# Pipelined attention scaling, ternary weights partly on ScalarE, and a per-block tile change in a one-layer transformer kernel

## The chip, the cores and the metric

The kernel runs on the eight cores of one Trainium2 chip. Each core takes half of the 4096 tokens of one of four batch items and computes its 2048 output rows alone; the keys and values of the whole item are computed on both of its cores. There is no exchange between cores. The metric is the device time in microseconds of the slowest core.

## The reference

One transformer layer with post-norm: linear attention, then a feed-forward network with ternary weights. Biases are zero, the norms have no gain.

```python
q = x @ Wq.T + bq;  k = x @ Wk.T + bk;  v = x @ Wv.T + bv   # 16 q heads, 4 kv heads, D = 128
sq, sk = elu(q) + 1, elu(k) + 1
kv = einsum('bhsd,bhse->bhde', sk, v);  k_sum = sk.sum(axis=2)
attn = einsum('bhsd,bhde->bhse', sq, kv) / (einsum('bhsd,bhd->bhs', sq, k_sum)[..., None] + 1e-6)
x = layernorm(x + attn @ Wo.T)
wq = lambda w: sign(w) * (abs(w) >= 0.7 * mean(abs(w)))      # 8192 x 2048 and 2048 x 8192
h = gelu(x @ wq(w1).T + b1, approximate=False)
x = layernorm(x + h @ wq(w2).T + b2)
```

## The kernel before

Each engine has an instruction list that is written in program order by `p.op`; every engine executes its own list strictly in order, and semaphores join them. `vector`, `scalar` and `gpsimd` operations also wait for the one before them on the same engine. Activations lie transposed: 128 of the 2048 model dimensions on the partitions (16 d blocks, `dc`), 512 tokens in the free dimension (4 tiles, `t`). DMAs are issued by SyncE (`dma("sync", ...)`: weights w1, w2, their quantised copies, y1s) and by GpSimd (`dma("gpsimd", ...)`: x, wq, wo, all writes), both in order. In the profile the line of a DMA issue is L192.

The stages, one behind the other:

1. K and V of all 4096 tokens and their product kv (L291 to L335), with part of the *scale jobs* beside it: `emit_scale` loads 512 KB of w1 or w2 and ScalarE sums absolute values (L262), VectorE adds them up (L269).
2. Q projection: 16 head blocks `ic`, 4 tiles `t` each. A block is 16 matmuls (L426), then two VectorE operations (L433, L436), Exp on ScalarE (L440) and an add (L442), which make `sq`. Behind them `emit_qkv(ic - 1, t)` multiplies the `sq` of the head before with kv: two matmuls (L382, and L385 for the norm row), Ln and Exp of that one row on ScalarE (L392, L398: the reciprocal), a matmul that spreads the row over 128 partitions (L401), a copy (L405) and the product (L411), into `arnB`. Eight scale jobs follow each `ic` while there are any, that is behind the first eight.
3. Output projection by 16 d blocks and 4 tiles (L553), residual, sums for the norm; the result y1 goes to DRAM (`y1s`). Then the norm's factors for the 4 tiles (L598 to L634).
4. For each tile `t`, the FFN. First the *first norm*: for each d block load y1s into `x1d`, multiply (L704), add (L710), cast to bf16 (L713). Then the first product, 64 chunks `fc` of 16 matmuls (L742), each followed by Gelu on ScalarE (L750). Then the second product, 16 d blocks of 64 matmuls (L790), each followed by the bias add (L799), the residual (L803) and the sums for the second norm (L810, L812, L817). Then that norm's factors (L820 to L855) and the *output norm*: per d block two VectorE operations (L863, L865), in place in `x1d`, and the DMA to `out`.

In the first tile the weights are quantised just ahead of their matmuls and written to DRAM (`w1q`, `w2q`); the other tiles load them from there. `quant_piece` does 128 x 512 weights: a load into one of four staging buffers, two VectorE operations (L677, L683) that make -1, 0 or 1, and the write. A chunk of w1 is 4 pieces and has two buffers, half a d block of w2 is 8 pieces and has three.

What decides the order around the change is the written order alone, in these places:

```python
            sq_toks[ic][t] = m4_
            if ic >= 1:
                emit_qkv(ic - 1, t)
...
            tld = dma("sync", x1d, y1s[t, dc],
                      waits=[y1_wr[t][dc], x1_free[dc],
                             wo_mm_done if t == 0 else None])
```

`x1_free[dc]` is the output DMA of the tile before: the load of y1s goes into the buffer that this DMA reads.

Of the kernel before, what the change touches and what calls it, by code (L numbers as in the profile page):

```python
# [112 lines left out]
def build_nc():  # L113
# [261 lines left out]
    def emit_qkv(ic, t):  # L375
        nonlocal qkv_free, nrm_free, rbc_free
        kvh = ic // 4
        kv_l = kvsb.ap()[:, kvh * 129: kvh * 129 + 128]
        ks_l = kvsb.ap()[:, kvh * 129 + 128: kvh * 129 + 129]
        sq_t = sq_tile(ic, t)  # L380
        tqkv = p.op("tensor", lambda e, o=PB[2].ap(), l=kv_l, r=sq_t:
                    e.matmul(o, l, r, start=True, stop=True),  # L382
                    waits=[sq_toks[ic][t], t_kv_ev, qkv_free], inc=sT)
        tnrm = p.op("tensor", lambda e, o=PB[3].ap()[0:1, :], l=ks_l, r=sq_t:
                    e.matmul(o, l, r, start=True, stop=True),  # L385
                    waits=[nrm_free], inc=sT)
        qkv_last_mm[ic] = tnrm
        j = (ic * NT + t) % 2
        u_r, r_r = row(0 + j), row(2 + j)
        tu = p.op("scalar", lambda e, o=u_r, a=PB[3].ap()[0:1, :],  # L390
                  b=c_eps_at.ap():
                  e.activation(o, a, AF.Ln, bias=b),  # L392
                  waits=[tnrm, uro[j], st_["c_eps_at"],
                         t_bkr if ic == 0 else None,
                         t_bvr if ic == 0 else None], inc=sC)
        nrm_free = tu
        tr = p.op("scalar", lambda e, o=r_r, a=u_r, s2=c_none.ap():
                  e.activation(o, a, AF.Exp, scale=s2),  # L398
                  waits=[st_["c_none"]], inc=sC)
        tbc = p.op("tensor", lambda e, o=PB[4].ap(), l=ones_k1.ap(), r=r_r:  # L400
# [142 lines left out]
    for dc in range(DC):  # L543
        for t in range(NT):
            par = (dc * NT + t) % 2
            two = None
            for icc in range(16):
# [7 lines left out]
                                  thr_done if (dc == 0 and t == 0) else None],  # L555
# [40 lines left out]
    for t in range(NT):  # L596
# [63 lines left out]
    def quant_piece(which, idx, pc512, dst, dram_dst, dst_waits):  # L660
        first = qres["rr"] == 0
        sl = qres["rr"] % 4
        bl = qres["rr"] % 2
# [12 lines left out]
        tb = p.op("vector", lambda e, o=btile, a=stage, b2=tneg:  # L676
                  e.tensor_single_scalar(o, a, b2, ALU.is_le),  # L677
                  waits=[tok_d, thr_done, qres["b_free"][bl],
                         sqprev if first else None,
                         abs_guard if first else None], inc=sV)  # L680
        qres["lastB"] = tb
        tqv = p.op("vector", lambda e, o=dst, a=stage, s2=tpos, b2=btile:
                   e.scalar_tensor_tensor(o, a, s2, b2, ALU.is_ge, ALU.subtract),  # L683
                   waits=[tb] + list(dst_waits), inc=sV)
# [254 lines left out]
```

How the kernel before makes its waits and increments, by code:

```python
                def go(eng):  # L95
                    for fn, waits, inc in self.ops[ename]:
                        for h, v in waits:
                            eng.wait_ge(h, v)
                        ins = eng.nop() if fn is None else fn(eng)
                        if inc is not None:
                            ins.then_inc(*inc)
```

## Time and profile before

| what | us |
|---|---|
| median of 3 runs | 4919.77 (4708.06 to 4966.57) |
| profiled execution | 4721.89 |
| its span, slowest core (5) | 4720.3 |
| spans of the other cores | 4686.0 to 4713.6 |
| busy PE / DVE / ACT / POOL | 3036.4 / 1587.1 / 730.4 / 420.0 |

The profile is one execution, on the slowest core; a busy time is a sum over all stages. PE is TensorE, DVE VectorE, ACT ScalarE, POOL GpSimd, SP SyncE. L426 is line 426 of the kernel. Matmul ends are modelled, and a sequence that is shown as one row (x16) is 16 instructions in a row.

### The profile page before, as it was taken

The page shows a single profiled execution, that of the slowest core. Times are in us where ns is not written, and L with a number is a line of the kernel's source. Part 1 is how long each engine was busy: PE and PEld are TensorE (multiplying, and loading weights), DVE is VectorE, ACT ScalarE, POOL GpSimd, SP SyncE. Part 2 cuts the span into 40 slices and gives each one's busy share as a digit, 9 for nine tenths or more (in the row PEclk, how much of TensorE's full clock was granted, in tenths as well). Part 3 has the DMA queues.
Part 4 walks back from the last instruction along what each step waited for, and adds up shares of the span by engine and source line. Part 5 has one row for each costly group of instructions (what it writes and reads, how often), then busy time and mean ns, then how long its engine had stood idle before and what let it go on. Part 6 is the DMA issues. An engine that isn't in the chain of part 4 may idle for free.

```text
span 4720.3 us, 40825 instructions; the slowest of 8 cores (4686.0 to 4720.3 us)
## 1 busy us (share of the span) xinstructions
PE 3036.4 (64%) x11722; PEld 1214.4 (26%) x11722; DVE 1587.1 (34%) x2744; ACT 730.4 (15%) x1153; POOL 420.0 (9%) x774
## 2 busy tenths in 40 slices
PE   2455545554776666356664444459995899949996
PEld 0122211111222222022221111124442334414442
DVE  0222222222333333466676656540025001140023
ACT  0344442332121000000000000001100110011100
POOL 1000000000000111022332222200000000000000
PEclk9667777776777888588887777779997999969998
DMA  9755562332011333178885555444443344334442
GB/s 171 177 173 171 178 183 80 89 83 61 13 25 32 98 102 99 60 200 211 222 237 179 180 162 168 144 147 143 156 152 125 125 139 165 134 125 139 156 153 106
DMA packets 215218, 644.51 MB, mean 137 GB/s; under 512 B 30674, under 2 KB 34770, under 8 KB 202708
## 3 DMA queue, kind: packets, MB, share of 16 engines
q1 hardware_dynamic: 161716, 486.66, 34.1%
q0 software_dynamic: 53280, 155.24, 11.7%
q8 instruction: 96, 1.57, 0.1%
q14 instruction: 126, 1.03, 0.1%
HBM read 578.87 MB, written 100.66 MB: 144 GB/s over the span
## 4 chain that ended last, share of the span: by engine, by line
PE 39%; DMA 25%; DVE 20%; ACT 7%; issue 6%; DVEq 1%; POOL 1%; ACTq 0%; SPq 0%; POOLq 0%
PE PB L790 17%; DMA arnE<-w 15%; PE PB L742 13%; PE PB L426 6%; DMA arnE<-xt 6%; DVE arnC L683 5%; DVE arnE L677 3%; ACT arnE L262 3%; DMA arnC<-w1q 2%; PE PB L401 2%; DVEq L98 1%; DVE arnE L433 1%; ACT rows L398 1%; DVE arnB L710 1%; DVE arnB L865 1%
## 5 line engine op out<-in xcount | busy, mean ns | idle before, releaser
L742 PE MATMUL PB<-arnB,arnC 128*128 128x512 bf16 x4096 | 987.9, 399 | 408.1 <-DVE arnC L683 206.4
L790 PE MATMUL PB<-arnA,arnC 128*128 128x512 bf16 x4096 | 939.2, 393 | 301.0 <-DVE arnC L683 301.0
L742 PEld LDWEIGHTS PB<-arnB,arnC 128*128 128x128 bf16 x4096 | 401.7, 101 | 998.6 <-issue 606.9
L790 PEld LDWEIGHTS PB<-arnA,arnC 128*128 128x128 bf16 x4096 | 410.5, 101 | 829.3 <-issue 382.2
L799 DVE TENSOR_SCALAR arnE<-PB,b_sb 128x512 f32<-128x512 f32 x64 | 48.0, 751 | 1370.0 <-PE PB L790 1370.0
L683 DVE SCALAR_TENSOR_TENSOR arnC<-arnE,thr 128x512 bf16<-128x512 f32 x512 | 384.8, 752 | 94.0 <-DVE arnE L677 32.4
L553 PE MATMUL PB<-arnB,arnC 128*128 128x512 bf16 x1024 | 272.7, 429 | 138.7 <-DVE arnE L568 138.7
L426 PE MATMUL PB<-arnA,arnC 128*128 128x512 bf16 x1024 | 336.7, 503 | 11.5 <-DMA arnC<-wq 9.7
L262 ACT ACTIVATE arnE<-arnE 128x1024 bf16<-128x1024 f32 x256 | 270.7, 1057 | 419.8 <-DMA arnE<-w 341.5
L750 ACT ACTIVATE arnA<-PB,b_sb 128x512 bf16<-128x512 f32 x256 | 176.3, 689 | 987.8 <-PE PB L742 987.8
L677 DVE TENSOR_SCALAR arnE<-arnE,thr 128x512 f32<-128x512 f32 x512 | 249.4, 487 | 124.2 <-DMA arnE<-w 78.9
L401 PE MATMUL PB<-rows,ones_k 1*128 1x512 f32 x128 | 94.6, 827 | 293.7 <-ACT rows L398 293.7
L269 DVE SCALAR_TENSOR_TENSOR acc<-acc_t,acc 128x1 f32<-128x1 f32 x256 | 40.8, 159 | 577.8 <-ACT arnE L262 573.5
L812 ACT ACTIVATE arnE<-arnB 128x512 f32<-128x512 f32 x64 | 40.4, 632 | 1206.0 <-DVE arnB L803 1206.0
L335 PE MATMUL PB<-arnG 128*128 128x129 bf16 x128 | 18.7, 301 | 297.1 <-DVE arnG L323 297.1
L426 PEld LDWEIGHTS PB<-arnA,arnC 128*128 128x128 bf16 x1024 | 121.3, 123 | 257.4 <-issue 212.3
L553 PEld LDWEIGHTS PB<-arnB,arnC 128*128 128x128 bf16 x1024 | 106.3, 108 | 306.1 <-issue 223.8
L192 POOL DMA_DIRECT2D out<-arnB x64 | 34.6, 540 | 1639.3 <-DVE arnB L865 1639.2
L192 POOL DMA_DIRECT2D w1q<-arnC x256 | 141.2, 552 | 416.9 <-DVE arnE L677 313.8
L192 POOL DMA_DIRECT2D w2q<-arnC x256 | 138.8, 542 | 434.6 <-DVE arnE L677 395.0
L568 DVE TENSOR_TENSOR arnE<-PB,arnE 128x512 f32<-128x512 f32 x64 | 44.2, 691 | 264.4 <-DMA arnE<-xt 250.2
L192 POOL DMA_DIRECT2D arnC<-wq x16 | 8.4, 528 | 1236.1 <-PE PB L385 654.1
(147 smaller groups left out, 1777.7 us busy)
## 6 DMA issues: line engine op xcount, KB each, us to landing
arnE<-w SPq DMA_DIRECT2D x256, 512.0 KB, 4.3
arnE<-w SPq DMA_DIRECT2D x512, 256.0 KB, 4.2
arnC<-w1q SPq DMA_DIRECT2D x192, 512.0 KB, 3.2
arnC<-w2q SPq DMA_DIRECT2D x96, 1024.0 KB, 5.0
w1q<-arnC POOLq DMA_DIRECT2D x256, 128.0 KB, 4.8
w2q<-arnC POOLq DMA_DIRECT2D x256, 128.0 KB, 3.4
arnE<-xt POOLq DMA_DIRECT2D x64, 256.0 KB, 3.7
y1s<-arnE POOLq DMA_DIRECT2D x64, 256.0 KB, 2.4
```

The costliest lines, as they stand in the source:

```text
L98: eng.wait_ge(h, v)
L192: tok = p.op(qeng, lambda e, a=dst, b=src: e.dma_start(out=a, in_=b), waits=list(waits) + [q["last"][i]], inc=q["lanes"][i], inc_amt=16)
L262: e.activation(Eb9, s2, AF.Abs, accum_out=a2),
L401: e.matmul(o, l, r, start=True, stop=True),
L426: e.matmul(o, l, r, start=s, stop=z),
L553: e.matmul(o, l, r, start=s, stop=z),
L677: e.tensor_single_scalar(o, a, b2, ALU.is_le),
L683: e.scalar_tensor_tensor(o, a, s2, b2, ALU.is_ge, ALU.subtract),
L742: e.matmul(o, l, r, start=s, stop=z),
L750: e.activation(o, a, AF.Gelu, bias=b),
L790: e.matmul(o, l, r, start=s, stop=z),
L799: e.tensor_scalar(o, a, b, None, ALU.add),
```

## The change

1. `emit_qkv` is split. The two matmuls, Ln and Exp stay (new L409, L414, and two ScalarE lines); the spreading matmul (L386), the copy and the product go into `emit_qkv_B`, which is called one block later, behind the next block's 16 matmuls and its VectorE operations. The two PSUM banks of `emit_qkv` become two pairs.
2. In `quant_piece`, one piece in four of w1 and three in eight of w2 take another form: Sign with bias -threshold and Sign with bias +threshold on ScalarE (L704, L708), their sum on VectorE (L711), and Sign of the sum on ScalarE (L713). All other pieces keep the two VectorE operations (L721, L725), with one scratch buffer in place of two. The matmuls wait for the last piece of either form.
3. The bias add of the second product moves from VectorE (L799) to ScalarE.
4. The first norm of tile t+1 is written block by block into the output norm of tile t: behind the two operations and the output DMA of d block `dc` come the load and the three operations (L747, L754, L757) of the same `dc`. Its scratch is Esl(1) instead of Esl(0).

```diff
@@ Q projection: emit_qkv split in two @@
-    qkv_free = nrm_free = rbc_free = None
+    qkv_free = [None, None]
+    nrm_free = [None, None]
+    rbc_free = None
...
+    qkv_pend = []
+    def emit_qkv_B():
+        nonlocal rbc_free
+        if not qkv_pend:
+            return
+        ic, t, qp, j, tqkv, tr = qkv_pend.pop(0)
+        tbc = p.op("tensor", lambda e, o=PB[4].ap(), l=ones_k1.ap(),
+                   r=row(2 + j):
                    e.matmul(o, l, r, start=True, stop=True),
                    waits=[tr, rbc_free], inc=sT)
...
-                   a=PB[2].ap(), b=Esl(0):
+                   a=PB[2 if qp == 0 else 5].ap(), b=Esl(0):
                    e.tensor_mul(o, a, b), waits=[tqkv], inc=sV)
-        qkv_free = tdv
+        qkv_free[qp] = tdv
...
+    def emit_qkv(ic, t):
...
+        qp = (ic * NT + t) % 2
+        tqkv = p.op("tensor", lambda e, o=PB[2 if qp == 0 else 5].ap(),
...
+                    waits=[sq_toks[ic][t], t_kv_ev, qkv_free[qp]], inc=sT)
+        tnrm = p.op("tensor",
+                    lambda e, o=PB[3 if qp == 0 else 6].ap()[0:1, :],
...
+        qkv_pend.append((ic, t, qp, j, tqkv, tr))
...
             sq_toks[ic][t] = m4_
+            emit_qkv_B()
             if ic >= 1:
                 emit_qkv(ic - 1, t)
...
     for t in range(NT):
+        emit_qkv_B()
         emit_qkv(15, t)
+    emit_qkv_B()
@@ quant_piece @@
-        btile = Esl(9) if bl == 0 else Esl(2)
...
+            cform = (pc512 % 4) == 1
...
+            cform = (pc512 % 8) in (1, 4, 6)
...
+        if cform:
...
+            s1 = Eb.ap()[:, 2048:2560]
+            s2 = Eb.ap()[:, 2560:3072]
+            ts1 = p.op("scalar", lambda e, o=s1, a=stage, b=tneg:
+                       e.activation(o, a, AF.Sign, bias=b),
+                       waits=[tok_d, thr_done,
+                              sqprev if firstC else None], inc=sC)
+            ts2 = p.op("scalar", lambda e, o=s2, a=stage, b=tpos:
+                       e.activation(o, a, AF.Sign, bias=b), inc=sC)
+            qres["stage_free"][sl] = ts2
+            tad = p.op("vector", lambda e, o=s1, a=s1, b=s2:
+                       e.tensor_add(o, a, b), waits=[ts2], inc=sV)
+            tqv = p.op("scalar", lambda e, o=dst, a=s1:
+                       e.activation(o, a, AF.Sign),
+                       waits=[tad] + list(dst_waits), inc=sC)
+            qres["lastB"] = tqv
+        else:
...
+            btile = Esl(9)
+            tb = p.op("vector", lambda e, o=btile, a=stage, b2=tneg:
+                      e.tensor_single_scalar(o, a, b2, ALU.is_le),
...
+            tqv = p.op("vector", lambda e, o=dst, a=stage, s2=tpos, b2=btile:
@@ first norm of a tile @@
+    def emit_ln1_dc(t, dc):
+        x1d = Bfap[:, dc * 512:(dc + 1) * 512]
+        x1b = Bbf[:, 16384 + dc * 512: 16384 + (dc + 1) * 512]
+        tld = dma("sync", x1d, y1s[t, dc],
+                  waits=[y1_wr[t][dc], x1_free[dc],
+                         wo_mm_done if t == 0 else None])
+        ta1 = p.op("vector", lambda e, o=Esl(1), a=x1d, b=Abc1(t):
+                   e.tensor_mul(o, a, b),
+                   waits=[tld, ab_done[t],
...
+        ta2 = p.op("vector", lambda e, o=x1d, a=Esl(1), b=Bbc1(t):
+                   e.tensor_add(o, a, b), inc=sV)
+        x1_ready[dc] = ta2
+        x1bf_ready[dc] = p.op("vector", lambda e, o=x1b, a=x1d:
+                              e.tensor_copy(o, a), inc=sV)
...
     for t in range(NT):
-        for dc in range(DC):
...
+        for dc in (range(DC) if t == 0 else []):
+            emit_ln1_dc(t, dc)
@@ bias add of the second product @@
-            tv1 = p.op("vector", lambda e, o=Esl(0), a=PB[2 + par].ap(),
+            tv1 = p.op("scalar", lambda e, o=Esl(0), a=PB[2 + par].ap(),
                        b=b2_sb.ap()[:, dc:dc + 1]:
-                       e.tensor_scalar(o, a, b, None, ALU.add),
-                       waits=[tmm, t_b2], inc=sV)
+                       e.activation(o, a, AF.Identity, bias=b),
+                       waits=[tmm, t_b2, ytmp_free], inc=sC)
@@ output norm @@
             x1_free[dc] = wr
             out_last = wr
             x1_ready[dc] = None
+            if t + 1 < NT:
+                emit_ln1_dc(t + 1, dc)
```

TensorE, Q projection, before (L382 and L385 are the two matmuls of `emit_qkv`, L401 spreads the row, L426 is the projection):

```order
L385 MATMUL PB3<-arnG,kvsb 1x512
L401 MATMUL PB4<-rows,ones_k1 128x512 [waits sC]
L426 MATMUL PB1<-arnA,arnC 128x512 x16
L382 MATMUL PB2<-arnG,kvsb 128x512 [waits sV]
L385 MATMUL PB3<-arnG,kvsb 1x512
L401 MATMUL PB4<-rows,ones_k1 128x512 [waits sC]
```

And now (L409, L414, L386 and L442 in the same roles):

```order
L442 MATMUL PB0<-arnA,arnC 128x512 x16
L386 MATMUL PB4<-rows,ones_k1 128x512 [waits sC,sV]
L409 MATMUL PB2<-arnG,kvsb 128x512 [waits sV]
L414 MATMUL PB3<-arnG,kvsb 1x512
L442 MATMUL PB1<-arnA,arnC 128x512 x16
L386 MATMUL PB4<-rows,ones_k1 128x512 [waits sC,sV]
L409 MATMUL PB5<-arnG,kvsb 128x512 [waits sV]
```

The 16 matmuls of the next block now stand between L409 and L414 and the L386 that belongs to them, and the two PSUM banks take turns with another pair.

ScalarE, first tile's first product, before, from the factors of the first norm to the residual's squares (L750 is Gelu):

```order
L614 ACTIVATE rows<-rows,c_eps_ln 1x512 [waits sV,sC]
L617 ACTIVATE rows<-rows,c_nhalf 1x512 [waits sC]
L750 ACTIVATE arnA<-PB,b_sb 128x512 [waits sT,sC] x64
L812 ACTIVATE arnE<-arnB 128x512 [waits sV,sG1,sC]
L812 ACTIVATE arnE<-arnB 128x512 [waits sV,sC] x15
```

And now (L806 is Gelu, L704 and L708 the two Signs, L713 the last one):

```order
L806 ACTIVATE arnA<-PB,b_sb 128x512 [waits sT,sC]
L704 ACTIVATE arnE<-arnE,thr 128x512 [waits sS2,sC]
L708 ACTIVATE arnE<-arnE,thr 128x512 [waits sC]
L713 ACTIVATE arnC<-arnE 128x512 [waits sV,sG0,sG1,sG2,sG3,sC]
L806 ACTIVATE arnA<-PB,b_sb 128x512 [waits sT,sC]
```

Between any two Gelus there now stand three Signs, of which the first waits for a weight load (sS) and the last for VectorE (sV) and for earlier writes (sG).

VectorE, first tile's first product, before, at its start (L710, L713 end the first norm; L677, L683 are a piece):

```order
L710 TENSOR_TENSOR arnB<-arnE,arnF 128x512 [waits sV]
L713 CAST arnB<-arnB 128x512 [waits sV]
L677 TENSOR_SCALAR arnE<-arnE,thr 128x512 [waits sS1,sV]
L683 SCALAR_TENSOR_TENSOR arnC<-arnE,thr 128x512 [waits sV]
L677 TENSOR_SCALAR arnE<-arnE,thr 128x512 [waits sS2,sV]
L683 SCALAR_TENSOR_TENSOR arnC<-arnE,thr 128x512 [waits sV]
```

And now (L721, L725 are a piece of the kept form, L711 the add of the new one):

```order
L754 TENSOR_TENSOR arnB<-arnE,arnF 128x512 [waits sV]
L757 CAST arnB<-arnB 128x512 [waits sV]
L721 TENSOR_SCALAR arnE<-arnE,thr 128x512 [waits sS1,sV]
L725 SCALAR_TENSOR_TENSOR arnC<-arnE,thr 128x512 [waits sV]
L711 TENSOR_TENSOR arnE<-arnE 128x512 [waits sC,sV]
L721 TENSOR_SCALAR arnE<-arnE,thr 128x512 [waits sS3,sV]
L725 SCALAR_TENSOR_TENSOR arnC<-arnE,thr 128x512 [waits sV]
L721 TENSOR_SCALAR arnE<-arnE,thr 128x512 [waits sS4,sV]
L725 SCALAR_TENSOR_TENSOR arnC<-arnE,thr 128x512 [waits sV]
```

Of each four pieces the second is now the one operation L711, which waits for ScalarE (sC); the third and fourth stand behind it.

VectorE, from the output norm of the first tile to the first norm of the second, before (L863, L865 output norm; L704, L710, L713 first norm):

```order
L863 TENSOR_TENSOR arnE<-arnB,arnE 128x512 [waits sV]
L865 TENSOR_TENSOR arnB<-arnE 128x512 [waits sV]
L704 TENSOR_TENSOR arnE<-arnB,arnF 128x512 [waits sS3,sV]
L710 TENSOR_TENSOR arnB<-arnE,arnF 128x512 [waits sV]
L713 CAST arnB<-arnB 128x512 [waits sV]
L704 TENSOR_TENSOR arnE<-arnB,arnF 128x512 [waits sS4,sV]
```

And now (L928, L930 output norm; L747, L754, L757 first norm):

```order
L928 TENSOR_TENSOR arnE<-arnB,arnE 128x512 [waits sV]
L930 TENSOR_TENSOR arnB<-arnE 128x512 [waits sV]
L747 TENSOR_TENSOR arnE<-arnB,arnF 128x512 [waits sS3,sV]
L754 TENSOR_TENSOR arnB<-arnE,arnF 128x512 [waits sV]
L757 CAST arnB<-arnB 128x512 [waits sV]
L928 TENSOR_TENSOR arnE<-arnB,arnE 128x512 [waits sV]
L930 TENSOR_TENSOR arnB<-arnE 128x512 [waits sV]
```

The three operations of the first norm, with the wait for their load (sS), have moved between the output norms of two neighbouring d blocks.

## Rows read from the trace of the kernel before

**Rows 1.** Busy time by stage: stretch, length, PE, PEld, DVE, ACT, POOL busy (instructions), clock, DMA, GB/s
```profile
...
690.00:1465.00 775.00, 452.43 (x1272) 154.85 (x1272) 239.58 (x401) 202.25 (x320) 9.00 (x17) 0.74 0.22 58
...
2010.00:2490.00 480.00, 296.40 (x1053) 112.83 (x1054) 335.42 (x542) 45.38 (x65) 148.22 (x270) 0.84 0.81 221
...
3366.00:3588.00 222.00, 221.20 (x1025) 100.10 (x1023) 44.00 (x63) 10.16 (x16) 0.00 (x0) 1.00 0.39 143
```

**Rows 2.** Timeline, Q projection: start, us, engine, line, operation, count [idle before <-releaser]
```profile
...
1258.95 0.72 ACT L398 ACTIVATE rows<-rows,c_none 1x512 f32<-1x512 f32 x1
...
1259.82 1.09 PE L401 MATMUL PB<-rows,ones_k 1*128 1x512 f32 x2 [2.92 <-ACT rows L398]
...
1260.84 5.31 PE L426 MATMUL PB<-arnA,arnC 128*128 128x512 bf16 x16
```

**Rows 3.** Chain that ended last, in order of time, Q projection: start, us, what
```profile
...
798.80 6.17 PE PB L426 x16
...
1140.66 5.91 PE PB L426 x16
...
1451.32 5.26 PE PB L426 x16
```

**Rows 4.** Timeline, TensorE, Q projection, end of a burst of scale jobs
```profile
...
907.81 2.04 PE L401 MATMUL PB<-rows,ones_k 1*128 1x512 f32 x2 [19.09 <-ACT rows L398]
```

**Rows 5.** Timeline, first FFN product of the first tile: first matmul, one chunk, last Gelu
```profile
...
2016.45 1.87 PE L742 MATMUL PB<-arnB,arnC 128*128 128x512 bf16 x4 [41.14 <-DVE arnC L683]
...
2223.87 5.30 PE L742 MATMUL PB<-arnB,arnC 128*128 128x512 bf16 x16 [2.11 <-DVE arnC L683]
...
2229.32 0.69 ACT L750 ACTIVATE arnA<-PB,b_sb 128x512 bf16<-128x512 f32 x1 [6.72 <-PE PB L742]
...
2471.93 0.69 ACT L750 ACTIVATE arnA<-PB,b_sb 128x512 bf16<-128x512 f32 x1 [3.48 <-PE PB L742]
```

**Rows 6.** Waits, 2100 to 2480 us: engine, tile, line <- releaser: us, times, longest
```profile
...
PE PB L742 <- DVE arnC L683: 136.3, 48, 4.9
```

**Rows 7.** Groups of instructions: line, engine, operation, shapes, count | busy, mean ns | idle before
```profile
...
L683 DVE SCALAR_TENSOR_TENSOR arnC<-arnE,thr 128x512 bf16<-128x512 f32 x512 | 384.8, 752 | 94.0 <-DVE arnE L677 32.4 <-DMA w2q<-arnC 9.5 <-DMA w1q<-arnC 8.4
L677 DVE TENSOR_SCALAR arnE<-arnE,thr 128x512 f32<-128x512 f32 x512 | 249.4, 487 | 124.2 <-DMA arnE<-w 78.9 <-DVE arnC L683 1.9
...
L812 ACT ACTIVATE arnE<-arnB 128x512 f32<-128x512 f32 x64 | 40.4, 632 | 1206.0 <-DVE arnB L803 1206.0
...
L750 ACT ACT_TABLE_LOAD x4 | 5.1, 1283 | 258.1 <-PE PB L742 258.1
```

**Rows 8.** Timeline, VectorE, second product of the first tile, two neighbouring bias adds
```profile
...
2611.22 0.75 DVE L799 TENSOR_SCALAR arnE<-PB,b_sb 128x512 f32<-128x512 f32 x1 [9.08 <-PE PB L790]
...
2648.00 0.75 DVE L799 TENSOR_SCALAR arnE<-PB,b_sb 128x512 f32<-128x512 f32 x1 [9.08 <-PE PB L790]
```

**Rows 9.** Timeline, from the second tile to the third
```profile
...
3608.03 0.69 DVE L863 TENSOR_TENSOR arnE<-arnB,arnE 128x512 f32<-128x512 f32 x1
3608.82 0.69 DVE L865 TENSOR_TENSOR arnB<-arnE 128x512 f32<-128x512 f32 x1
...
3613.29 26.38 SPq L192 DMA_DIRECT2D arnB<-y1s  x16
...
3667.29 0.43 DVE L713 CAST arnB<-arnB 128x512 bf16<-128x512 f32 x1
...
3667.86 4.39 PE L742 MATMUL PB<-arnB,arnC 128*128 128x512 bf16 x12 [1.54 <-DVE arnB L713]
```

**Rows 10.** Time to landing: out and y1s by tile, 3600 to 3672 us; page, part 6
```profile
...
DMA to landing us min/median/max: 3.0/4.8/6.6
...
DMA to landing us min/median/max: 2.9/4.3/5.2
...
arnE<-w SPq DMA_DIRECT2D x512, 256.0 KB, 4.2
...
y1s<-arnE POOLq DMA_DIRECT2D x64, 256.0 KB, 2.4
```

More of the change, by code:

```diff
@@ L373, in build_nc @@
     thr_done = None
[L375 to L400, printed above, removed]
+    qkv_pend = []
[6 more added lines that the diff above has]
+                   r=row(2 + j):
                    e.matmul(o, l, r, start=True, stop=True),
@@ L409, in emit_qkv @@
                    o=Bbf[:, ic * 2048 + t * 512: ic * 2048 + (t + 1) * 512],
-                   a=PB[2].ap(), b=Esl(0):
+                   a=PB[2 if qp == 0 else 5].ap(), b=Esl(0):
                    e.tensor_mul(o, a, b), waits=[tqkv], inc=sV)
-        qkv_free = tdv
+        qkv_free[qp] = tdv
         if t == NT - 1:
             attnT_tok[ic] = tdv
+    def emit_qkv(ic, t):
+        kvh = ic // 4
+        kv_l = kvsb.ap()[:, kvh * 129: kvh * 129 + 128]
+        ks_l = kvsb.ap()[:, kvh * 129 + 128: kvh * 129 + 129]
+        sq_t = sq_tile(ic, t)
+        qp = (ic * NT + t) % 2
+        tqkv = p.op("tensor", lambda e, o=PB[2 if qp == 0 else 5].ap(),
+                    l=kv_l, r=sq_t:
+                    e.matmul(o, l, r, start=True, stop=True),
+                    waits=[sq_toks[ic][t], t_kv_ev, qkv_free[qp]], inc=sT)
+        tnrm = p.op("tensor",
+                    lambda e, o=PB[3 if qp == 0 else 6].ap()[0:1, :],
+                    l=ks_l, r=sq_t:
+                    e.matmul(o, l, r, start=True, stop=True),
+                    waits=[nrm_free[qp]], inc=sT)
+        qkv_last_mm[ic] = tnrm
+        j = (ic * NT + t) % 2
+        u_r, r_r = row(0 + j), row(2 + j)
+        tu = p.op("scalar", lambda e, o=u_r,
+                  a=PB[3 if qp == 0 else 6].ap()[0:1, :],
+                  b=c_eps_at.ap():
+                  e.activation(o, a, AF.Ln, bias=b),
+                  waits=[tnrm, uro[j], st_["c_eps_at"],
+                         t_bkr if ic == 0 else None,
+                         t_bvr if ic == 0 else None], inc=sC)
+        nrm_free[qp] = tu
+        tr = p.op("scalar", lambda e, o=r_r, a=u_r, s2=c_none.ap():
+                  e.activation(o, a, AF.Exp, scale=s2),
+                  waits=[st_["c_none"]], inc=sC)
+        qkv_pend.append((ic, t, qp, j, tqkv, tr))
     for ic in range(16):
@@ L675, in quant_piece @@
                            stats_guard if first else None])
[L676 to L684, printed above, removed]
@@ L727, in build_nc @@
                     wtoks.append(tw)
-                w1q_tok[par] = tqv
+                    if cf:
+                        clast = tqv
+                    else:
+                        vlast = tqv
+                w1q_tok[par] = [x for x in (vlast, clast) if x is not None]
                 gwr_w1[par] = wtoks
             else:
-                w1q_tok[par] = dma(
+                w1q_tok[par] = [dma(
                     "sync", buf, w1q[fc],
-                    waits=[w1q_free[par]] + qres["wr_w1"][fc] + gwr_w1[par])
+                    waits=[w1q_free[par]] + qres["wr_w1"][fc] + gwr_w1[par])]
                 gwr_w1[par] = []
@@ L742, in build_nc @@
                           e.matmul(o, l, r, start=s, stop=z),
-                          waits=[w1q_tok[par], x1bf_ready[dc], h_free[par]],
+                          waits=w1q_tok[par] + [x1bf_ready[dc],
+                                                h_free[par]],
                           inc=sT if dc == DC - 1 else None)
```

74 lines of the change are left out of this document (43 added, 31 removed).

## The prediction

> **What bounds the kernel now.** I read the busy time by stage first, then single cycles. TensorE has the most busy time, but no stage waits for the same thing, so a share of the whole span says little. In three stretches of it [rows 1], the Q projection (690 to 1465 us) runs at a granted clock of 0.74, the quantising pass of the first token tile has VectorE busy for 335 of 480 us with DMA at 0.81, and the second FFN product of a later tile is all TensorE: 1025 matmuls in 221.2 us, 216 ns each, clock 1.00. That last row is the price of a matmul at the full level (2.4 GHz); at the lower level (1.2 GHz) it is double, 0.43 us.
>
> In the Q projection the reader is to see a chain that goes round the engines for every block: the matmul L401 starts 2.92 us late because it waits for ScalarE's L398, and only behind it in TensorE's order come the next 16 matmuls, 5.31 us of them, where 16 x 0.216 = 3.5 us would do: the idle time brings the lower clock for part of each block [rows 2]. The chain of waits gives the pace: 798.80 to 1140.66 us are six output blocks with a burst of scale jobs each, 57.0 us apiece; 1140.66 to 1451.32 us are 30 blocks without one, 10.4 us each, 41.4 us for four [rows 3]. In a burst TensorE stands for 19.09 us [rows 4], since Exp of the next block is queued on ScalarE behind eight Abs.
>
> In the quantising pass, first product (I call it G1), the first matmul starts at 2016.45 and the last Gelu ends at 2472.62 us: 456 us for 64 chunks, 7.1 us each [rows 5]. TensorE waits there for VectorE's L683 [rows 6]. VectorE can run ahead of TensorE, because nothing in its own work of a chunk waits for Gelu. In the second product (G2) of that tile the bias add L799 comes every 36.8 us [rows 8].
>
> Between tiles VectorE is alone: 16 times two operations of the output norm (1.59 us), then 16 times three of the next tile's first norm (2.12 us), from 3608.03 to 3667.86 us. 16 x (1.59 + 2.12) = 59.4 fills these 59.8 us, so no load of y1s is waited for; the first goes out at 3613.29 us, under the loop [rows 9]. An operation is counted to the start of the next: L863 to the second L863 is 1.59 us, of the three two are alike and the Cast takes 0.43 and a gap of 0.1.
>
> **Part 1, the Q projection: gain.** B of a block (L401 and the two VectorE operations) now stands behind the next block's 16 matmuls, and its ScalarE rows have long been done. TensorE's own cycle is 16 x 0.216 = 3.5, plus 1.0 for L401 (from its start at 1259.82 to the next at 1260.84), plus 2 x 0.216 and handovers, some 0.6, for the two small matmuls: 5.1 us. VectorE has five operations of 0.7 to 0.75 us, about 4.1 us with gaps, ScalarE three: both shorter than 5.1. Quiet blocks: 4 x 5.1 = 20.4 against 41.4 us, eight times: -168. With a burst, some 20 us of ScalarE stay (TensorE's 19.09 [rows 4] less the usual 2.92, and about 4 us of matmuls that still run under it); behind it, Exp chain 3.5, L401 at the lower clock 2.0, the small pair 1.2, then two blocks of 16 with their small matmuls, about 14: some 41 instead of 57, eight times: -128. The last four blocks have no projection to hide in, and I give them -4. Sum -300. Bounds: if the clock stays at the lower level, a block is 16 x 0.43 + 2.0 + 1.0 = 9.9 us and the quiet part gains next to nothing (total -60); if all overlaps, -340. I take the full clock, because TensorE has no waits of its own left and the gapless stage shows 1.00 [rows 1].
>
> **Part 2, G1 of the first tile: loss.** One piece in four (L704 to L713 of the new kernel) becomes Sign, Sign, an add on VectorE, Sign. VectorE saves 1.45 us (0.49 + 0.75 and gaps [rows 7]) and pays one add. But ScalarE executes in order: the two Signs of chunk n+1 stand behind Gelu of chunk n, which waits for the matmuls of chunk n; and on VectorE the pieces 2 and 3 of chunk n+1 stand behind the add, which waits for those Signs. The cycle closes: Gelu end, two Signs 1.6 us (0.69 to 0.72 each, nearest row Square at 0.63 without a pointer operand), add 0.6 with its waits, two pieces 2.9, 16 matmuls 5.3 to 5.4 (they start cold as now [rows 5]), Gelu 0.15 + 0.69. That is 11.3 us against 7.1: 64 x 4.2 = +267. Bounds: matmuls at the full clock and the add at 0.43 (the Cast L713, half 16-bit [rows 9]), 9.6 us, +160; all matmuls at the lower clock, 13.2 us, +390. DMA is no limit then: the same bytes in 1.6 times the time, and the share was 0.81. The bf16 add has no row; between 0.43 (Cast) and 0.69 (the fp32 adds) I took 0.43 plus its waits.
>
> For this add the Trainium skill ("VectorE: DVE Perf Modes", section "Mode 2×_1P — pack two bf16 into one 32-bit read") says that a tensor-tensor operation whose operands are all 16 bit makes two results a cycle. That would be about 0.3 us, an estimate from its 0.96 GHz, and 64 x 0.13 = 8 us less; no row of this trace shows one.
>
> **Part 3, G2 of the first tile: small gain.** Six of 16 pieces leave VectorE for ScalarE, which waits for no Gelu here. VectorE's part falls from 16 x 1.45 = 23.2 to 10 x 1.45 + 6 x 0.6 = 18.1 us, but the loads then set the pace: four stages, each held 1.45 us and 4.2 us in landing (median [rows 10]), are 1.4 us a piece. So I count 2 us of each 36.8 as gained, -35 in 16. Bounds -60 (the full VectorE relief less the waits for the add) and +20 (ScalarE's third Sign late for the second half's matmuls). Moving the bias add to ScalarE costs and gains about nothing: 0.69 instead of 0.75 and one more handover.
>
> **Part 4, between tiles: the large loss.** L747 to L757 of the next tile now stand on VectorE right behind the output norm of the same d block. The load of y1s writes the buffer that the output DMA has just read, so it waits for that DMA to finish; VectorE waits for the load, and the next d block's output norm is queued behind. Nothing is in flight for the next block, as its output has not been computed. The price: the first L865 ends at 3609.51, SyncE issues the first y1s load at 3613.29 [rows 9], 3.8 us later; the load takes at least 2.9 us, in the median 4.3, to land [rows 10]. A block is 1.59 + 3.8 + 3.2 + 0.1 + 2.12 = 10.8 instead of 3.7 us; sixteen: +113. Then 12 or so matmuls of chunk 0 run cold behind the last block, which were hidden before: +5. Three times: +354. Bounds: a write as fast as those of y1s (2.4 us, and 0.6 to issue it) and the fastest load (2.9) make 9.8 us a block, +300; the medians of out and y1s (4.8 and 4.3) 13 us, +460.
>
> Sum: -300 + 267 - 35 + 354 = +286. The profiled execution took 4721.9 us (span 4720.3 and 1.6 around it): 5008 us. The median of the three runs, 4919.8, stands 4.2% above that execution, the lowest 0.3% below; a run that is as much longer would be at 5218.
>
> **Rivals.** (a) The gate of Part 2 does not bind, for instance if ScalarE passes the Signs before Gelu. For it: in the before the pieces run ahead of Gelu. Against it: the order of the program. G1 then stays at 7.1 us: 5008 - 267 = 4741, within 2%, the other side. It decides from the point where the cycle without Gelu, about 7 us, is the longest. (b) The round trips of Part 4 are hidden. For it: y1s costs VectorE nothing today. Against: every link is a wait on one buffer. 5008 - 354 = 4654, 1.4% faster. (c) Part 1 doesn't do what it says, since the clock stays at the lower level with the bursts around: -60 instead of -300, 5248. (d) Sign and Gelu need different tables, and each chunk reloads twice: 64 x 2 x 1.283 us [rows 7] = +164, 5172. Against it: Square runs between the Gelus of two tiles and the page has just one load per tile and line.
>
> On (d) the Trainium skill ("ScalarE: Activation LUTs", section "Table sets: the hidden batching unit") says that each switch of set costs a table load, and that cheap functions like relu, copy and abs are in every set; Sign is not named in that sentence. The trace agrees with its rule for Square and with its 1283 ns.
>
> **Chances.** Forecast 0.77, (a) 0.07, (b) 0.04, (c) 0.08, (d) 0.04. About 2% is what a measurement of this kernel can tell from no change: below 4628 or above 4816. Slower takes forecast, (c), (d), less 0.01 for a forecast whose losses all lie at their low bounds: 0.88. Within 2%: 0.10, from (a), most of (b) and that 0.01. Faster: 0.02, half of (b). The bounds of all parts will not all fall on one side: the distances to the low ones (40, 107, 25, 54) make 129 as the root of their squares, which puts the low end at 4880. The high end, 5240, takes in (d), the run 4.2% longer (5218) and nearly (c).
>
> **What would show it.** Right: no wait of L386 for the reciprocal in quiet blocks and clock near 1 there; in G1 a Gelu every 11 us with TensorE waiting for VectorE's last piece, VectorE waiting for ScalarE at the add; between tiles VectorE idle for 7 us before each L747 by the y1s DMA, the stage 60 to 175 us long. Wrong: a G1 pace under 9 us, a tile change under 120 us, or table loads among the Signs.

## The result and the profile after

The changed kernel takes 5107.31 us in the median (5085.28 to 5323.76) beside 4769.3 us (4701.33 to 4992.92) of the kernel before on the same chip: ratio 1.0824, 95% interval 1.0797 to 1.085. The forecast was 5008 us, within 4880 to 5240. In some executions, of either kernel, the cores of one die ran at a lower clock and took longer; the ratios, the single times and the row of e4 in the table of stages leave them out, the medians of all executions do not.

The page of after, the slowest core (4); the median over the cores is 5077.6 us on one die and 5079.0 us on the other. The second row of the fence is busy time by engine:

```profile
span 5104.9 us, 42451 instructions; the slowest of 8 cores (5054.6 to 5104.9 us)
...
PE 3007.5 (59%) x11722; PEld 1206.9 (24%) x11722; DVE 1410.0 (28%) x2520; ACT 1104.5 (22%) x1697; POOL 420.8 (8%) x774
```

VectorE lost 177 us of work, ScalarE gained 374, TensorE's work hardly moved, and the span is 385 us longer: less work on the busiest helper and more waiting. The ledger by stage, core 5 before and core 4 after. Each of the first four rows starts where the row above it ends:

| stage | before | after | difference | forecast |
|---|---|---|---|---|
| start to first output projection matmul | 1489.2 | 1227.6 | -262 | -300 |
| to first G1 matmul | 527.3 | 529.4 | +2 | 0 |
| G1 of the first tile, to its last Gelu | 456.2 | 761.4 | +305 | +267 |
| G2 of the first tile, to its last bias add | 576.1 | 597.4 | +21 | -35 |
| three tile changes with the G1 behind each, from last bias add to first G2 matmul | 957.2 | 1274.7 | +317 | +354 |

The same stages by window, after (stretch, length, busy us and instructions of PE, PEld, DVE, ACT, POOL, clock, DMA share, GB/s): Q projection, G1, G2, a tile change, G2 of the second tile. They answer to [rows 1].

```profile
693.00:1227.00 534.00, 368.22 (x1286) 132.32 (x1286) 244.57 (x408) 206.81 (x326) 9.01 (x17) 0.81 0.31 82
1757.00:2518.00 761.00, 365.68 (x1024) 127.07 (x1024) 261.99 (x443) 175.40 (x254) 139.45 (x256) 0.71 0.46 133
2543.00:3107.00 564.00, 268.30 (x961) 105.38 (x962) 257.30 (x438) 206.31 (x300) 132.69 (x241) 0.72 0.53 167
3136.00:3293.00 157.00, 0.06 (x1) 0.09 (x1) 50.35 (x79) 0.00 (x0) 8.64 (x16) 0.50 0.18 60
3394.00:3615.00 221.00, 211.64 (x965) 92.23 (x964) 11.35 (x17) 33.31 (x49) 0.00 (x0) 1.00 0.43 150
```

Three things are to be seen. The Q projection has a higher clock, 0.81. In G1 neither any engine nor the DMA is busy half the time, which is what a chain that goes round would give. In the tile change almost nothing runs for 157 us.

**Q projection.** The timeline of TensorE after, quiet blocks (start, us, engine, line, operation, count, idle before). L386 is what L401 was [rows 2]:

```profile
1190.46 1.12 PE L386 MATMUL PB<-rows,ones_k 1*128 1x512 f32 x2
...
1192.14 3.63 PE L442 MATMUL PB<-arnA,arnC 128*128 128x512 bf16 x16
...
1195.70 1.12 PE L386 MATMUL PB<-rows,ones_k 1*128 1x512 f32 x2
```

L386 has no idle time in front, the 16 matmuls take 3.63 us instead of 5.31, and a block is 5.24 us. The granted clock of the quiet blocks is 1.00 (1035 to 1190 us) where it was 0.80 (1145 to 1450 us before). Two burst ends [rows 4], 42.5 us apart:

```profile
863.37 2.04 PE L386 MATMUL PB<-rows,ones_k 1*128 1x512 f32 x2 [18.00 <-DVE arnE L390]
...
905.90 2.04 PE L386 MATMUL PB<-rows,ones_k 1*128 1x512 f32 x2 [17.46 <-DVE arnE L390]
```

**G1.** One chunk on the timeline after [rows 5]: the 16 matmuls, Gelu (L806), the two Signs (L704, L708), the add (L711), the next VectorE piece, the next matmuls:

```profile
1783.22 5.10 PE L797 MATMUL PB<-arnB,arnC 128*128 128x512 bf16 x16 [6.22 <-DVE arnC L725]
...
1788.47 0.69 ACT L806 ACTIVATE arnA<-PB,b_sb 128x512 bf16<-128x512 f32 x1 [7.41 <-PE PB L797]
1789.25 0.72 ACT L704 ACTIVATE arnE<-arnE,thr 128x512 bf16<-128x512 f32 x1
1790.07 0.72 ACT L708 ACTIVATE arnE<-arnE,thr 128x512 bf16<-128x512 f32 x1
1790.96 0.42 DVE L711 TENSOR_TENSOR arnE<-arnE 128x512 bf16<-128x512 bf16 x1 [6.20 <-ACT arnE L708]
1791.49 0.49 DVE L721 TENSOR_SCALAR arnE<-arnE,thr 128x512 f32<-128x512 f32 x1
...
1794.54 1.86 PE L797 MATMUL PB<-arnB,arnC 128*128 128x512 bf16 x4 [6.22 <-DVE arnC L725]
```

Each row starts within 0.3 us of where the one before ends (two VectorE pieces fit between 1791.49 and 1794.54); the Signs show no wait for their weights, only for their place behind Gelu. The waits after, 1800 to 2500 us (us, times, longest), answer to [rows 6]:

```profile
ACT arnA L806 <- PE PB L797: 473.6, 59, 8.9
DVE arnE L711 <- ACT arnE L708: 402.2, 59, 7.8
PE PB L797 <- DVE arnC L725: 368.6, 59, 6.6
```

In every one of the 59 chunks three engines wait in turn for one another.

**Tile change.** The chain of waits after, one block and the start of the next, where before all three VectorE operations followed without a gap [rows 9]:

```profile
3136.46 0.70 DVE arnB L930
...
3137.78 2.66 DMA out<-arnB
3140.55 2.63 DMA arnB<-y1s
...
3143.34 0.70 DVE arnE L747
...
3147.57 2.65 DMA out<-arnB
3150.34 2.82 DMA arnB<-y1s
```

The write to `out`, then the load of y1s into the same buffer, 16 times; the loop takes 3135.66 to 3293.4 us, 157.8 instead of 59.8. In the three tile changes it takes 157.8, 161.7 and 157.5 us. The waits of that stretch:

```profile
DVE arnE L747 <- DMA arnB<-y1s: 100.1, 16, 6.8
```

**G2.** The bias adds are 37.6 us apart in the mean of 15 (before 36.6). The waits after, 2560 to 3100 us:

```profile
DVE arnB L865 <- ACT arnE L861: 138.3, 14, 11.1
...
DVE arnE L711 <- ACT arnE L708: 96.4, 63, 3.1
ACT arnE L704 <- DMA arnE<-w: 77.8, 55, 3.1
```

### The profile page after: what moved, and what is told of

The parts are those of the page before. It is cut to its first block, busy times and chain, and to the rows that moved or that the text cites. A ratio compares the mean times of both kernels' runs of the same rounds, so it can differ in the third digit from the quotient of the medians.

```text
span 5104.9 us, 42451 instructions; the slowest of 8 cores (5054.6 to 5104.9 us)
## 1 busy us (share of the span) xinstructions
PE 3007.5 (59%) x11722; PEld 1206.9 (24%) x11722; DVE 1410.0 (28%) x2520; ACT 1104.5 (22%) x1697; POOL 420.8 (8%) x774
## 4 chain that ended last, share of the span: by engine, by line
PE 41%; DMA 26%; DVE 15%; ACT 9%; issue 7%; DVEq 1%; POOL 1%; ACTq 0%; SPq 0%; POOLq 0%
PE PB L797 18%; PE PB L852 16%; DMA arnE<-w 11%; DMA arnE<-xt 5%; PE PB L442 4%; DMA arnC<-w1q 3%; DVE arnC L725 3%; ACT arnE L262 3%; DMA out<-arnB 3%; DMA arnB<-y1s 2%; DVE arnE L721 2%; ACT arnE L704 2%; ACT arnE L708 2%; PE PB L386 1%; DVE arnE L711 1%
## 5 line engine op out<-in xcount | busy, mean ns | idle before, releaser
L797 PE MATMUL PB<-arnB,arnC 128*128 128x512 bf16 x4096 | 1054.6, 420 | 963.4 <-DVE arnC L725 435.2
L852 PE MATMUL PB<-arnA,arnC 128*128 128x512 bf16 x4096 | 949.5, 396 | 312.2 <-DVE arnC L725 295.4
L852 PEld LDWEIGHTS PB<-arnA,arnC 128*128 128x128 bf16 x4096 | 412.8, 101 | 848.6 <-issue 407.7
L865 DVE TENSOR_TENSOR arnB<-arnE,arnB 128x512 f32<-128x512 f32 x64 | 44.3, 692 | 1452.6 <-ACT arnE L861 1452.6
L806 ACT ACTIVATE arnA<-PB,b_sb 128x512 bf16<-128x512 f32 x256 | 175.9, 687 | 1091.7 <-PE PB L797 1091.7
L572 PE MATMUL PB<-arnB,arnC 128*128 128x512 bf16 x1024 | 272.9, 428 | 139.6 <-DVE arnE L589 137.7
L725 DVE SCALAR_TENSOR_TENSOR arnC<-arnE,thr 128x512 bf16<-128x512 f32 x352 | 264.5, 751 | 78.1 <-DVE arnE L721 42.4
L442 PE MATMUL PB<-arnA,arnC 128*128 128x512 bf16 x1024 | 247.7, 399 | 13.2 <-DMA arnC<-wq 9.5
L711 DVE TENSOR_TENSOR arnE<-arnE 128x512 bf16<-128x512 bf16 x160 | 68.0, 425 | 545.6 <-ACT arnE L708 542.8
L861 ACT ACTIVATE arnE<-PB,b_sb 128x512 f32<-128x512 f32 x64 | 44.0, 687 | 710.6 <-PE PB L852 710.6
L721 DVE TENSOR_SCALAR arnE<-arnE,thr 128x512 f32<-128x512 f32 x352 | 172.5, 490 | 41.4 <-DMA arnE<-w 3.0
L386 PE MATMUL PB<-rows,ones_k 1*128 1x512 f32 x128 | 81.8, 722 | 132.9 <-DVE arnE L390 106.0
L713 ACT ACTIVATE arnC<-arnE 128x512 bf16<-128x512 bf16 x160 | 100.7, 630 | 203.3 <-DVE arnE L711 144.0
L704 ACT ACTIVATE arnE<-arnE,thr 128x512 bf16<-128x512 f32 x160 | 115.5, 722 | 106.8 <-DMA arnE<-w 97.5
```

Source lines behind the costliest of these rows:

```text
L442: e.matmul(o, l, r, start=s, stop=z),
L572: e.matmul(o, l, r, start=s, stop=z),
L704: e.activation(o, a, AF.Sign, bias=b),
L711: e.tensor_add(o, a, b), waits=[ts2], inc=sV)
L797: e.matmul(o, l, r, start=s, stop=z),
L806: e.activation(o, a, AF.Gelu, bias=b),
```

## The experiments

The median over the cores, in us, of four stretches: Q projection and G1 of the first tile, each from its first matmul to the first matmul of the next stage, G2 of the first tile, from its first matmul to the first output norm, and "rest", from there to the last matmul of the last tile. The kernels e5, e7 and e8 were run again as e11, e10 and e9, which stand here:

| kernel | Q projection | G1 | G2 | rest |
|---|---|---|---|---|
| before | 787.5 | 454.4 | 588.6 | 1598.9 |
| after | 533.4 | 772.1 | 605.8 | 1907.9 |
| e1 part 1 alone | 533.6 | 443.2 | 592.6 | 1603.4 |
| e2 without part 4 | 533.0 | 773.4 | 605.2 | 1604.2 |
| e3 without Sign pieces | 532.7 | 453.0 | 595.4 | 1906.4 |
| e4 first norm four blocks late (cores 4 to 7) | 533.9 | 771.9 | 606.2 | 1610.1 |
| e6 Sign piece last | 534.0 | 663.1 | 606.2 | 1906.0 |
| e11 pieces ahead of Gelu | 534.8 | 495.0 | 609.2 | 1915.8 |
| e10 both repairs | 534.1 | 494.2 | 610.8 | 1625.4 |
| e9 part 1, w2 pieces ahead | 532.8 | 457.3 | 466.0 | 1612.5 |

**e1: before with part 1 alone** (the first part of the diff above and nothing of the rest).

> The kernel before with part 1 alone (B of a block behind the next block's 16 matmuls). Theory: the stages are one behind the other and their gains add, so this gives what the two traces show up to the first matmul of the output projection, -262 us: ratio to the kernel before 0.944, some 4457 us. Rival: part of the 262 us comes from the rest of the change, or the earlier end of this stage is given back in the next (output projection waits, colder clock): a ratio of 0.955 or more.

Measured: 4467.16 us in the median, ratio 0.943 (0.9376 to 0.9484). The whole gain of the change is in part 1, and it stands on its own. The G1 of e1 is the same work as before's, 443 us instead of 454: G1 without Sign pieces lies between 443 and 464 us in before, e1, e3, e8 and e9 (medians over the cores), so 10 us of G1 tell nothing.

**e2: after without part 4.**

```diff
-        for dc in (range(DC) if t == 0 else []):
+        for dc in range(DC):
...
-            if t + 1 < NT:
-                emit_ln1_dc(t + 1, dc)
```

> The changed kernel with part 4 undone: the first norm of the next tile stands behind the whole output norm again. Theory: VectorE's wait for the round trip (write out, load y1s) is the whole price, and it goes: each tile change back to 60 us, -317 us against the changed kernel, ratio to the kernel before 1.082 - 0.067 = 1.015. Rival: the tile change is long for another reason too (w1q loads that are issued late, cold matmuls of chunk 0), then only 16 x 6.2 x 3 = 298 us or less go and the ratio stays at 1.02 or above.

Measured: 1.0144 (1.011 to 1.0178), 4799.13 us. Only "rest" moves: of the 309 us that it had grown, 304 go, 101 a tile change. That is nearer to the rival's 298 us than to the 317 of the theory; the ratio is the theory's.

**e3: after with every piece in the VectorE form.**

```diff
-            cform = (pc512 % 4) == 1
+            cform = False
...
-            cform = (pc512 % 8) in (1, 4, 6)
+            cform = False
```

> The changed kernel with every piece in the two-operation VectorE form (part 2 and the pieces of part 3 undone, bias add still on ScalarE). Theory: the first product of the first tile goes back from 11.9 to 7.1 us a chunk (-305) and the second from 37.6 to 36.6 us a block (-21): ratio to the kernel before 1.082 - 0.069 = 1.013. Rival: the bias add on ScalarE carries the loss of the second product, then only -305, ratio 1.018, and its pitch stays at 37.6.

Measured: 4794.34 and 4799.02 us, beside 4714 to 4744 us of before: about 1.4% more. G1 returns from 772 to 453 us and G2 from 606 to 595: the Sign pieces cost some 10 us in G2, too, where they were to gain. G2 doesn't return the 21 us of the theory.

**e4: after, the first norm four d blocks behind the output norm.** The order still interleaves the two norms, but the round trip of a block has four blocks of time.

```diff
-            if t + 1 < NT:
+            if t + 1 < NT and dc >= 4:
+                emit_ln1_dc(t + 1, dc - 4)
+        if t + 1 < NT:
+            for dc in range(DC - 4, DC):
                 emit_ln1_dc(t + 1, dc)
```

> The changed kernel with the first norm of d block n written behind the output norm of d block n+4 instead of n. Theory: a round trip of 6.2 + 1.6 us fits under four blocks of 3.7 us (14.9 us), so VectorE no longer waits and the tile change is 60 us as before: ratio 1.015, as with the norms apart. Rival: it is the mixing of writes and loads on the DMA queues, not the order on VectorE, that costs; then some of the wait stays, with a ratio between 1.03 and 1.08.

Measured: 1.0195 (1.0105 to 1.0285). The timeline of VectorE in a tile change of e4, core 4:

```profile
3161.47 0.69 DVE L928 TENSOR_TENSOR arnE<-arnB,arnE 128x512 f32<-128x512 f32 x1
3162.26 0.69 DVE L930 TENSOR_TENSOR arnB<-arnE 128x512 f32<-128x512 f32 x1
3163.06 0.69 DVE L747 TENSOR_TENSOR arnE<-arnB,arnF 128x512 f32<-128x512 f32 x1
3163.85 0.69 DVE L754 TENSOR_TENSOR arnB<-arnE,arnF 128x512 f32<-128x512 f32 x1
```

L747 starts 0.11 us after L930 ends; in after it waited 6.2 us. In all three tile changes of this core L747 waits 4.8 us for y1s, in after 100.1 us in the first alone. So the loss of part 4 is the round trip over one buffer, not the mixing of the two loops, and four blocks of distance hide it.

**e5 and e11: after, with the pieces of chunk n+1 written ahead of the matmuls and Gelu of chunk n.** The same work, in an order where the Signs don't stand behind the Gelu that waits for their neighbours.

```diff
+        if t == 0:
+            quant_chunk(0)
...
-                for pc in range(4):
...
+                if fc + 1 < NFC:
+                    quant_chunk(fc + 1)
```

> The changed kernel, but in the first tile the four pieces of chunk n+1 are written ahead of the matmuls and the Gelu of chunk n; nothing else changes, the Signs stay. Theory: the loss of the first product is the gate by ScalarE's order alone, so it goes: 454 us from the first chunk's matmul to the first matmul of the second product instead of 772, -318 us, ratio to the kernel before 1.082 - 0.067 = 1.015. Rival: the four operations of a Sign piece in a row over two engines (2.8 us of work, four handovers) are what makes a chunk long; then the product stays above 600 us and the ratio above 1.045.

> The kernel of e5_pieces_ahead once more, for an interval. Theory (only the gate in G1 is taken away, 772 - 487 = 285 us of 5080): ratio 1.0824 - 285/4720 = 1.022. Rival (G1 gate not the cause): 1.08.

Measured: e5 4829.5 and 4865.25 us, with G1 near 487; e11, the same kernel on another chip, 1.0189 (1.0138 to 1.0241), G1 495. The gate is real: the order alone gives back 277 of 318 us. It does not give back all, as the theory of e5 had it. The waits of e11, core 4, 1850 to 2200 us:

```profile
PE PB L805 <- DVE arnC L725: 128.4, 45, 4.8
ACT arnE L704 <- DMA arnE<-w: 125.9, 47, 4.6
DVE arnE L711 <- ACT arnE L708: 68.2, 48, 3.2
```

ScalarE's first Sign now waits for its weights, and VectorE's add for ScalarE. What sets the pace of e11's chunks (495/64 = 7.7 us, against 7.1) is probably a load and two handovers; no run takes these apart.

**e6: after, with the Sign piece last of the four.** The pieces that VectorE makes alone then stand ahead of the add.

```diff
-            cform = (pc512 % 4) == 1
+            cform = (pc512 % 4) == 3
```

> The changed kernel with the Sign piece of a w1 chunk in the last place of four instead of the second. Theory of the gate: the Signs still wait for Gelu, but the three VectorE pieces now run ahead of it. The cycle is 16 matmuls 5.7, Gelu 0.84, two Signs 1.6, add 0.6, third Sign 0.85, 9.6 us instead of 11.9: the product takes some 620 us instead of 772, ratio 1.05. Rival (the Sign piece's own work is the price, wherever it stands): 772 us as before, ratio 1.08.

Measured: 4990.12 and 4993.68 us, G1 663.1 us instead of the 620 expected. The timeline of e6, core 3, TensorE:

```profile
2002.11 6.03 PE L797 MATMUL PB<-arnB,arnC 128*128 128x512 bf16 x16 [4.21 <-ACT arnC L713]
2012.34 6.03 PE L797 MATMUL PB<-arnB,arnC 128*128 128x512 bf16 x16 [4.21 <-ACT arnC L713]
```

and ScalarE:

```profile
2008.29 0.69 ACT L806 ACTIVATE arnA<-PB,b_sb 128x512 bf16<-128x512 f32 x1 [6.33 <-PE PB L797]
2009.07 0.72 ACT L704 ACTIVATE arnE<-arnE,thr 128x512 bf16<-128x512 f32 x1
2009.88 0.72 ACT L708 ACTIVATE arnE<-arnE,thr 128x512 bf16<-128x512 f32 x1
2011.57 0.63 ACT L713 ACTIVATE arnC<-arnE 128x512 bf16<-128x512 bf16 x1 [0.96 <-DVE arnE L711]
```

The cycle is Gelu, two Signs, add, Sign, 16 matmuls: 10.23 us. The two VectorE pieces have left it (TensorE's idle time falls from 6.22 to 4.21 us), so the loop is the one named. The size was missed, 9.6 us expected: the matmuls took 6.03 us and not 5.7, and from the end of the second Sign to the start of the third it was 0.97 us and not 0.6.

**e7 and e10: after with both repairs**, e4's and e5's. Does ScalarE's relief of VectorE pay once nothing is gated?

> The changed kernel with both repairs: pieces of chunk n+1 ahead of Gelu n, and the first norm four blocks behind the output norm. Theory: both losses go and the gain of part 1 stays: -318 - 309 us against the changed kernel, ratio 0.95. The work that left VectorE is then worth nothing, since loads set the pace in both products. Rival: with VectorE relieved the first product gets faster than the kernel before's 454 us (VectorE was busy 316 of 457 us), ratio below 0.94.

> The kernel of e7_repaired once more, for an interval. Theory (the relief of VectorE by ScalarE is worth nothing, some handovers stay): ratio 0.955 to 0.960, that is above e1's 0.943. Rival (the relief pays once nothing is gated): 0.93 or less.

Measured: e7 4520.29 us; e10 0.9552 (0.9488 to 0.9615), 4566.01 us in the median. That is above e1's 0.943, though VectorE has 176 us less to do. Taking that work from it gained nothing: G1 is 494 and G2 611 us, both longer than with VectorE alone (443 to 464 and 589 to 595). Another 22 us of the difference to e1 lie in "rest", not in the two products.

**e8 and e9: before with part 1, and w2 pieces ahead of the bias add.** Of the first tile's second product, the first half of the next d block's pieces is written ahead of this block's bias add, the second half behind its sums, so that VectorE doesn't wait at the bias add with nothing to do.

```diff
+        if t == 0:
+            load_half(0, 0)
+            load_half(0, 1)
...
+            if t == 0 and dc + 1 < DC:
+                load_half(dc + 1, 0)
             tv1 = p.op("vector", lambda e, o=Esl(0), a=PB[2 + par].ap(),
...
+            if t == 0 and dc + 1 < DC:
+                load_half(dc + 1, 1)
```

> The kernel before with part 1, and in the second product of the first tile the first half of the next block's pieces is written ahead of the bias add and sums of this block, on VectorE. Theory: VectorE waits 9.1 us a block there for the matmuls of the second half (L799), which is an order on the engine like the two that this change made; with pieces to do it is filled until the loads set the pace: 6.3 MB a block at the 221 GB/s of the first product is 28.5 us instead of 36.6, -120 us of 589, ratio 0.943 - 0.026 = 0.917. Rival: the loads set the pace already in the second product, 1.45 us a piece and no more; then it stays at 0.943.

> The kernel of e8_split_w2_ahead once more, on another chip and with more rounds, for an interval beside the kernel before. Theory (the first half of the next d block's w2 pieces ahead of the bias add keeps VectorE and the loads busy while TensorE works): ratio 0.921, G2 near 468 us. Rival (the gain of e8 over e1, 0.022, was that chip's): ratio 0.943 as in e1.

Measured: e8 4342.68 us and e9 4384.12 us in the median; e9's ratio 0.9176 (0.9126 to 0.9226). It beats both kernels, and e1. The windows of G2, e1 (core 4), then e9 (core 5):

```profile
2200.00:2600.00 400.00, 189.39 (x677) 75.41 (x692) 244.84 (x391) 6.93 (x11) 93.95 (x172) 0.73 0.54 170
```

```profile
2170.00:2580.00 410.00, 259.79 (x923) 101.57 (x922) 326.43 (x521) 11.68 (x18) 127.22 (x235) 0.81 0.74 226
```

VectorE's busy share goes from 0.61 to 0.80 and DMA from 0.54 to 0.74. The waits of the same stretches, e1, then e9:

```profile
PE PB L811 <- DVE arnC L704: 212.2, 22, 16.8
DVE arnE L820 <- PE PB L811: 96.1, 11, 9.1
```

```profile
PE PB L820 <- DVE arnC L704: 138.5, 27, 8.5
...
DVE arnE L698 <- DMA arnE<-w: 15.9, 28, 1.8
```

In e1 the bias add (L820) holds VectorE for 8.7 us in each block; among e9's waits it is not found. The gain over e1, 127 us of G2, is what parts 2 and 3 looked for in VectorE's work and the order had instead.

## Why the prediction was right, and where its terms were off

The sign, the two losses and the two mechanisms behind them were right: e1 isolates part 1, e2 and e4 part 4, e3 and e11 part 2. In ratios, 1.0824 less 0.0629 (e4) less 0.0635 (e11) is 0.956, and the kernel with these two repairs measures 0.9552: the parts add up. The forecast was 99 us low against the median, of which the ledger's lines make 97 (38 + 2 + 38 + 56 - 37). Four lines erred by 134 us to one side; that 37 came back from part 4 was luck.

- **Part 1, -300; measured -262.** The quiet block (5.1 forecast, 5.24 by the row, 5.3 in the mean) and the period with a burst (41 forecast; 740.77 to 1031.86 us in the chain are seven, 41.6 each) were right, and the clock rose as chosen: rival (c) is out. The gains were counted too often. The first head has no `emit_qkv`, so its burst block, with 16 us of gain, had nothing to give: 696.26 to 742.42 us before, 693.09 to 740.77 after. And between 1140.66 and 1451.32 us [rows 3] lie 31 blocks, not 30: a quiet block was 10.02 us, four 40.1, and 32 of them gain 320.7 - 170.8 = 150 instead of 168. The last four blocks gain 3.
- **Part 2, +267; measured +305.** The cycle was right link by link (a wait at the add, a wait for the last VectorE piece, 59 times in 59 chunks), and rivals (a) and (d) are out. Both bounds of the prediction are 0.35 us above what its own links add up to (9.2 and 12.8 us, or +136 and +366); with them the low end of the range would be some 20 us lower. The mean chunk is 761.4/64 = 11.9 us, not 11.3. TensorE's share of it, in the group of its matmuls from 1757 to 2518 us:

```profile
L797 PE MATMUL PB<-arnB,arnC 128*128 128x512 bf16 x1024 | 365.7, 535 | 435.2 <-DVE arnC L725 435.2
```

  365.7/64 = 5.7 us busy (forecast 5.3 to 5.4, from one row of before), and 6.22 us idle (forecast 5.95). The 16 matmuls are the term that was mis-sized most: 64 x 0.35 = 22 of the 38 us. They took 444 ns each in the mean before and 535 after, with more waiting and a granted clock of 0.71 instead of 0.84.
- **Part 3, -35; measured +21.** The step that failed is "2 us of each 36.8 as gained" (16 times 2 is 32, by the way, not 35). VectorE's sum did fall, but it was not what held a block: before, 129.2 us in 15 blocks went to VectorE's wait for the second half's matmuls at the bias add, which part 2 leaves in place (138.3 us in 14 blocks after, now at L865 behind ScalarE), and each Sign piece adds a wait for its load and one for the add. "ScalarE, which waits for no Gelu here" overlooked the bias add that part 3 itself had moved there: ScalarE waits 135.0 us in 14 blocks at it (L861) for the matmuls, and the next block's Signs stand behind it. e3 puts 10 us of the loss on the Sign pieces; the other 7 of the medians' 17, for the bias add on ScalarE, are not shown: e1, without it, has 4 us more than before on another chip, and e3 only 3 us more than e1 on the same one. e9 shows the price of the wait itself: 127 us.
- **Part 4, +354; measured +317.** The mechanism held: 16 waits, 6.3 us each in the mean. The write and the load were sized from a busy stretch, 3.8 us from L865 to the first load's issue and 3.2 us to land [rows 9, 10]; in the emptied stretch, with DMA at 0.18, the write takes 2.66 and the load 2.63 us, 3.4 and 2.8 us with what stands around them. So a block is 9.86 us (low bound 9.8), and the loop 98 to 102 us longer instead of 113. The matmuls behind it and the rest cost some 6 us a change, forecast 5. Rival (b) is out.

Rival (d) in the groups of after: ScalarE loads its table for Gelu four times, once a tile, as before. Of the 160 Signs of each kind 64 stand among the Gelus of G1, the other 96 in G2.

```profile
L711 DVE TENSOR_TENSOR arnE<-arnE 128x512 bf16<-128x512 bf16 x160 | 68.0, 425 | 545.6 <-ACT arnE L708 542.8
...
L713 ACT ACTIVATE arnC<-arnE 128x512 bf16<-128x512 bf16 x160 | 100.7, 630 | 203.3 <-DVE arnE L711 144.0
L704 ACT ACTIVATE arnE<-arnE,thr 128x512 bf16<-128x512 f32 x160 | 115.5, 722 | 106.8 <-DMA arnE<-w 97.5
...
L806 ACT ACT_TABLE_LOAD x4 | 5.1, 1283 | 527.7 <-PE PB L797 527.7
```

So Sign needs no set of its own beside Gelu. The Trainium skill ("ScalarE: Activation LUTs", section "Table sets: the hidden batching unit") says that each switch of set costs a load and that cheap functions are in every set; the trace fits it if Sign is counted among these, which that section doesn't name.

The bf16 add took 425 ns, the 0.43 that was chosen, and the 8 us that the prediction set aside for it did not come. The fp32 additions of the same size take 692 ns (L928, L930), 267 ns more. The Trainium skill ("VectorE: DVE Perf Modes", section "Mode 2×_1P — pack two bf16 into one 32-bit read") says that such an add makes two results a cycle, and the trace agrees: 267 ns are 256 cycles at the page's 0.96 GHz, half of the 512 results. What was wrong is the prediction's 0.3 us, an estimate from that page that counted only the results; by the two rows some 160 ns of each operation stay whatever the type.

## What to carry to other kernels

Work that is moved to an engine with spare time moves into that engine's order: write down what stands ahead of it there and what that waits for, all the way round, before its duration counts. A load into a buffer that is just being written out needs a distance of some blocks (four were enough here), and the price of the round trip was set by the DMA's speed when alone, not by the medians of the busy stretch next to it. And where a helper engine is idle once per block at a wait for the main engine, moving its next work ahead of that wait gave more (127 us) than taking a quarter to three eighths of its pieces away (nothing).

## What the runs showed of the hardware beyond that

- In the tile change the same transfers of 256 KB land in 2.6 to 2.7 us where the busy stretch had 4.3 and 4.8 [rows 10].
- The granted clock followed TensorE's gaps in both directions: 0.74 to 0.81 in the Q projection, where the waits of TensorE vanished in quiet blocks, 0.84 to 0.71 in G1, where they grew, and 0.50 in the tile change, where it had nothing to do. Removing a stall paid twice in the first (16 matmuls 5.31 to 3.63 us), adding one cost twice in the second (a matmul 444 to 535 ns in the mean).
- In G1 after, with the same 6.22 us idle before each chunk, the 16 matmuls take 5.0 to 5.2 us and 6.2 to 6.3 us in turn (2152.88: 6.28, 2165.38: 5.16, 2176.77: 6.29). Why they alternate was not tried.
